# The last feed-forward of a four-layer decoder: one phase over all groups, the second weight quantised inside it, the result stored row by row

## The reference

```python
def fake_quant_weight(w, bits=8):
    qmax = 2.0 ** (bits - 1) - 1
    scale = jnp.max(jnp.abs(w)) / qmax
    return jnp.clip(jnp.round(w / scale), -qmax - 1, qmax) * scale

def qat_lora_linear(x, W, b, A, B):
    base = jnp.einsum('bsi,oi->bso', x, fake_quant_weight(W)) + b
    lora = jnp.einsum('bsr,or->bso', jnp.einsum('bsi,ri->bsr', x, A), B)
    return base + 2.0 * lora

h = qat_lora_linear(layernorm(x), W_fc, b_fc, A_fc, B_fc)          # 256 -> 1024
h = jax.nn.gelu(h, approximate=False)
x = x + qat_lora_linear(h, W_proj, b_proj, A_proj, B_proj)         # 1024 -> 256
```

## Time and profile before

| | us |
|---|---|
| median of 3 runs (3753.2 to 3757.0) | 3754.8 |
| the profiled execution | 3752.83 |
| its span, first to last instruction | 3751.0 |
| TensorE busy | 3235.7 (86%) |
| VectorE busy | 2180.4 (58%) |
| ScalarE busy | 1803.9 (48%) |
| GpSimd busy | 1012.5 (27%) |
| mean granted TensorE clock | 0.913 |

### The profile page before, as it was taken

How to read it: one execution, slowest core, us unless ns; L and a number is a source line. 1 busy time by engine, 2 the same in 40 slices (tenths; PEclk the granted TensorE clock), 3 DMA queues, 4 the chain that set the end, 5 groups by cost and what they waited for, 6 DMA issues and landing times. The chain is left out here.

```text
span 3751.0 us, 54988 instructions
## 1 busy us (share of the span) xinstructions
PE 3235.7 (86%) x18722; PEld 1868.1 (50%) x18722; DVE 2180.4 (58%) x4483; ACT 1803.9 (48%) x4177; POOL 1012.5 (27%) x1177
## 2 busy tenths in 40 slices
PE   6978639998859899967899989795899999998988
PEld 3655428887637566634455556363233333332745
DVE  5764445455555565575645447334788888884730
ACT  5956613333223244443544435212477777776521
POOL 2534544433421022232344332104011111111300
PEclk9988759999979899988888889897799999999989
DMA  9100045665430000042000031213100000001100
GB/s 336 56 9 1 1 195 189 204 190 170 146 93 2 12 1 1 1 131 80 1 1 1 1 140 53 108 55 123 39 13 14 18 18 18 18 10 47 46 0 23
DMA packets 160866, 240.51 MB, mean 64 GB/s; under 512 B 22531, under 2 KB 135812, under 8 KB 156708
## 3 DMA queue, kind: packets, MB, share of 16 engines
q1 hardware_dynamic: 146772, 199.27, 16.2%
q0 software_dynamic: 13824, 37.77, 3.1%
HBM read 131.97 MB, written 104.99 MB: 63 GB/s over the span
## 5 line engine op out<-in xcount | busy, mean ns | idle before, releaser
L4145 DVE TENSOR_REDUCE peaks<-ps 128x1 f32<-128x1024 f32 x512 | 609.0, 1221 | 149.3 <-PE ps L4091 144.0
L4173 ACT ACTIVATE attn<-ps 128x512 f32<-128x512 f32 x1024 | 536.6, 604 | 117.4 <-PE ps L4082 115.8
L4091 PE MATMUL ps<-keys,queries 96*128 96x512 bf16 x1024 | 396.9, 393 | 19.2 <-DMA keys<-parts 15.5
L4082 PE MATMUL ps<-queries,keys 99*128 99x512 bf16 x1024 | 390.4, 385 | 3.5 <-ACT attn L4173 2.7
L4104 PE MATMUL ps<-attn,head_values 128*32 128x512 f32 x2048 | 272.3, 604 | 0.0
L4082 PEld LDWEIGHTS ps<-queries,keys 99*128 99x128 bf16 x1024 | 99.1, 98 | 307.0 <-ACT attn L4173 222.7
L1930 PE MATMUL ps<-experts,tileT 128*128 x884 | 231.4, 384 | 5.2 <-issue 5.2
L1145 POOL TENSOR_TENSOR attn_w<-attn_w,attn_share 128x512 f32<-128x512 f32 x128 | 130.7, 1042 | 377.3 <-DVE attn_share L1014 377.3
L2133 DVE COPY normed<-ps 128x256 f32<-128x256 f32 x221 | 93.8, 424 | 205.7 <-PE ps L1946 108.1
L1848 POOL DMA_INDIRECT rows<-expert_rows,index x128 | 121.6, 950 | 197.8 <-DVE normed L2133 115.0
L1946 PE MATMUL ps<-experts,hiddenT 128*128 (+1 forms) x474 | 147.5, 393 | 28.9 <-DVE hiddenT L2142 25.3
(11 more groups left out here) (653 smaller groups left out, 7049.4 us busy)
## 6 DMA issues: line engine op xcount, KB each, us to landing
tile_in<-routed_rows SPq DMA_DIRECT2D x244, 128.0 KB, 2.2
expert_rows<-normed SPq DMA_DIRECT2D x221, 128.0 KB
routed_rows<-zeros SPq DMA_DIRECT2D x2, 8064.0 KB, 44.9
experts<-in_L_ffn_experts SPq DMA_DIRECT2D x4, 3072.0 KB
routed_rows<-zeros SPq DMA_DIRECT2D x1, 12160.0 KB, 61.2
kT<-L_xattn_keys SPq DMA_DIRECT2D x8, 1024.0 KB
v<-L_xattn_values SPq DMA_DIRECT2D x8, 1024.0 KB
experts<-in_L_ffn_experts SPq DMA_DIRECT2D x8, 1024.0 KB
```

The source lines that it names most:

```text
L4082: nc.tensor.matmul(bank(("score", n)), keys[h % 3][0:DEEP, sl(kt)], queries[h % 3][0:DEEP, sl(c, CHUNK)], start=True, stop=True).then_inc( ...
L4091: last = nc.tensor.matmul(k.ps[:, SB + p % PB, :], queries[h % 3][0:ROWS, sl(t)], keys[h % 3][0:ROWS, sl(c, CHUNK)], start=True, stop=True)
L4145: v.tensor_reduce(peaks[:, r % 2, i // 2, i % 2:i % 2 + 1], k.ps[:, at:at + 2, :], AX.XY, ALU.max).then_inc(s["maxed"], 1)
L4173: nc.scalar.activation(attn[:, n % RING, :], bank(("score", n)), ACT.Exp, scale=1.0 / 16.0).then_inc(s["read"], 1)
```

## The change

`l3_ffn` becomes one phase, "feed", with a program written out for each engine. The land phase, the quantise phase, the eight phases of the groups and the store phase in `build` are gone, and no loop is left.

- TensorE makes the four low-rank products of W_fc as soon as the weights are there, then turns and spreads the maximum of W_fc alone, transposes group 0 and makes its "up" products. For each later group g it makes all 8 transposes, then the "up" products of g, then the "down" products of g-1. In group 1 the maximum of W_proj is turned and spread and its eight low-rank products stand one behind each "up" product.
- VectorE takes the maximum of W_fc, the statistics of group 0, normalises it, quantises W_fc and adds its low-rank products; then the statistics of the other 12 rows at once, the maximum of W_proj, the normalising of group 1, and then it quantises W_proj and adds its low-rank products. Behind that it normalises group g+2 and adds the four rows of group g.
- ScalarE takes two roots (group 0; the other 12 rows, between the fifth and the sixth Gelu of group 0), copies both halves of the transposed group in one operation, and makes the Gelus. `hT` and `xT` exist twice.
- SyncE stores each of the 16 rows (128 KB) as soon as it is added, and waits for all at the end.
- "up" products go to banks 0 to 3, "down" and low-rank ones of W_proj to 4 and 5, transposes to 6 and 7. The bias product stands first in each "down" row instead of last.

```diff
@@ -2543,6 +2543,8 @@
     nc = k.nc
     INNER, RANK = 1024, 16
     M = INNER // P
+    CHUNK = 512
+    UP, DOWN, TURN = (0, 1, 2, 3), (4, 5), (6, 7)
     n = "L3_ffn_"
...
@@ -2553,74 +2555,211 @@
...
-        side_by_side(k, (land_part(k), 1))
...
-        LORA = [(0, kt, c) for kt in range(KD) for c in range(INNER // 512)] + [(1, m, 0) for m in range(M)]
...
-        side_by_side(k, (quantise, 1), (norm_part(k, 0, lambda kt: k.xT[:, kt, :], (4, 5)), 1))
...
-        def group(g, more):
-            gemm_phase(k, "up", [(P, GT, products([(wf[:, kt, sl(m)], k.xT[:, kt, :]) for kt in range(KD)]), "act", to_gelu(m))
-                                 for m in range(M)])
-            side_by_side(k, (gemm_part(k, "down", residual_jobs(k, g, hT, M, wp, bp), range(4)), 1),
-                         *([(norm_part(k, g + 1, lambda kt: k.xT[:, kt, :], (4, 5)), 1)] if more else []))
...
+        hT = [sb(k, stack, f"hT{i}", [P, M, GT]) for i in range(2)]
+        xT = [k.xT, sb(k, stack, "xT", [P, KD, GT])]
+        size, row_ = sb(k, stack, "size", [P, 2, 3]), sb(k, stack, "row", [1, 2, 2])
+        stats, moments = sb(k, stack, "stats", [P, BATCH, 6]), sb(k, stack, "moments", [P, BATCH, 2])
+        rstd = sb(k, stack, "rstd", [P, BATCH])
+        LORA_UP = [(kt, h) for h in range(INNER // CHUNK) for kt in range(KD)]
+        out = k.out.rearrange("b t d -> t b d")
+        names = ("step peaked turned maxed spread sized up_lora up_ready down_lora down_ready measured rooted normed xturned x_took "
+                 "up_made gelu_done down_made added stored")
+        with phase(k, "feed", names) as (block, s):
+            @block.sync
+            def _(sp):
+                fetch_next(k, sp)
+                for t in range(BATCH):
+                    sp.wait_ge(s["added"], t + 1)
+                    sp.dma_start(out[:, t, :], k.x[:, t, :]).then_inc(s["stored"], 16)
+                sp.wait_ge(s["stored"], 16 * BATCH)
+            @block.tensor
+            def _(pe):
...
+                def turn(g):
+                    if g >= 1:
+                        pe.wait_ge(s["x_took"], g)
+                    for j in range(GROUP):
+                        pe.wait_ge(s["normed"], g * GROUP + j + 1)
+                        for kt in range(KD):
+                            last = nc.tensor.transpose(k.ps[:, TURN[kt], sl(j)], k.normed[:, j, sl(kt)], k.ident[:, :])
+                    last.then_inc(s["xturned"], 1)
+                def lora_up(i):
+                    kt, h = LORA_UP[i]
+                    nc.tensor.matmul(k.ps[:, UP[i], :], af[:, sl(kt)], bfT[:, sl(h, CHUNK)], start=True, stop=True).then_inc(s["up_lora"], 1)
+                def lora_down(m):
+                    if m >= 2:
+                        pe.wait_ge(s["down_ready"], m - 1)
+                    else:
+                        pe.wait_ge(s["sized"], 2)
+                    nc.tensor.matmul(k.ps[:, DOWN[m % 2], 0:DIM], ap[:, sl(m)], bpT[:, :], start=True, stop=True).then_inc(s["down_lora"], 1)
+                def up(g, m):
+                    at = g * M + m
+                    if m == 0:
+                        pe.wait_ge(s["x_took"], g + 1)
+                    if g == 0 and m < 4:
+                        pe.wait_ge(s["up_ready"], 4 if m == 3 else max(2, m + 1))
+                    if at >= 4:
+                        pe.wait_ge(s["gelu_done"], at - 3)
+                    if g == 0 and m == 4:
+                        pe.wait_ge(s["up_ready"], 4)
+                    for kt in range(KD):
+                        last = nc.tensor.matmul(k.ps[:, UP[at % 4], :], wf[:, kt, sl(m)], xT[g % 2][:, kt, :], start=kt == 0, stop=kt == KD - 1)
+                    last.then_inc(s["up_made"], 1)
+                def down(g, j):
+                    at = g * GROUP + j
+                    if at == 0:
+                        pe.wait_ge(s["down_ready"], M)
+                    if at >= 2:
+                        pe.wait_ge(s["added"], at - 1)
+                    bank = k.ps[:, DOWN[at % 2], 0:DIM]
+                    nc.tensor.matmul(bank, k.ones[0:1, 0:P], bp[0:1, :], start=True, stop=False)
+                    for m in range(M):
+                        if j == 0:
+                            pe.wait_ge(s["gelu_done"], g * M + m + 1)
+                        last = nc.tensor.matmul(bank, hT[g % 2][:, m, sl(j)], wp[:, m, :], start=False, stop=m == M - 1)
+                    last.then_inc(s["down_made"], 1)
+                landed(k, pe)
+                for i in range(len(LORA_UP)):
+                    lora_up(i)
+                turn_peaks(0)
+                spread(0)
+                turn(0)
+                for m in range(M):
+                    up(0, m)
+                for g in range(1, GROUPS):
+                    turn(g)
+                    if g == 1:
+                        turn_peaks(1)
+                    for m in range(M):
+                        up(g, m)
+                        if g == 1:
+                            if m == 0:
+                                spread(1)
+                            else:
+                                lora_down(m - 1)
+                    if g == 1:
+                        lora_down(M - 1)
+                    for j in range(GROUP):
+                        down(g - 1, j)
+                for j in range(GROUP):
+                    down(GROUPS - 1, j)
+            @block.vector
+            def _(dve):
+                link = Link(dve, s["step"])
+                v = nc.vector
+                both = (wf, wp)
...
+                def peak_of_all(which):
+                    dve.wait_ge(s["turned"], which + 1)
+                    link(v.tensor_reduce(row_[:, which, 0:1], k.ps[0:1, DOWN[0], 0:P], AX.X, ALU.max))
+                    v.tensor_scalar(row_[:, which, 1:2], row_[:, which, 0:1], 1.0 / 127.0, None, ALU.mult).then_inc(s["maxed"], 1)
+                def quantise(which):
+                    w = both[which]
+                    dve.wait_ge(s["spread"], which + 1)
+                    v.tensor_copy(size[:, which, 1:2], k.ps[:, DOWN[1], 0:1]).then_inc(s["sized"], 1)
+                    dve.wait_ge(s["sized"], which + 1)
+                    link(v.reciprocal(size[:, which, 2:3], size[:, which, 1:2]))
+                    link(v.tensor_scalar(w[:, :, :], w[:, :, :], size[:, which, 2:3], MAGIC, ALU.mult, ALU.add))
+                    link(v.tensor_scalar(w[:, :, :], w[:, :, :], MAGIC, 127.0, ALU.subtract, ALU.min))
+                    link(v.tensor_scalar(w[:, :, :], w[:, :, :], -128.0, size[:, which, 1:2], ALU.max, ALU.mult))
+                def measure(tiles):
...
+                    link(v.tensor_scalar(rstd[:, these], moments[:, these, 1], LN_EPS, None, ALU.add))
+                    v.reciprocal(rstd[:, these], rstd[:, these]).then_inc(s["measured"], 1)
+                def normalise(g):
+                    dve.wait_ge(s["rooted"], min(g, 1) + 1)
+                    if g >= 1:
+                        dve.wait_ge(s["xturned"], g)
+                    for j in range(GROUP):
+                        t = g * GROUP + j
+                        v.tensor_scalar(k.normed[:, j, :], k.x[:, t, :], moments[:, t, 0:1], rstd[:, t:t + 1],
+                                        ALU.subtract, ALU.mult).then_inc(s["normed"], 1)
+                def add(g, j):
+                    t = g * GROUP + j
+                    dve.wait_ge(s["down_made"], t + 1)
+                    v.tensor_tensor(k.x[:, t, :], k.ps[:, DOWN[t % 2], 0:DIM], k.x[:, t, :], ALU.add).then_inc(s["added"], 1)
+                landed(k, dve)
+                peak(0)
+                measure(range(GROUP))
+                peak_of_all(0)
+                normalise(0)
+                quantise(0)
+                for i, (kt, h) in enumerate(LORA_UP):
+                    dst = wf[:, kt, sl(h, CHUNK)]
+                    dve.wait_ge(s["up_lora"], i + 1)
+                    v.scalar_tensor_tensor(dst, k.ps[:, UP[i], :], 2.0, dst, ALU.mult, ALU.add).then_inc(s["up_ready"], 1)
+                measure(range(GROUP, BATCH))
+                peak(1)
+                normalise(1)
+                peak_of_all(1)
+                quantise(1)
+                for m in range(M):
+                    dve.wait_ge(s["down_lora"], m + 1)
+                    v.scalar_tensor_tensor(wp[:, m, :], k.ps[:, DOWN[m % 2], 0:DIM], 2.0, wp[:, m, :], ALU.mult, ALU.add).then_inc(s["down_ready"], 1)
+                for g in range(GROUPS):
+                    if g + 2 < GROUPS:
+                        normalise(g + 2)
+                    for j in range(GROUP):
+                        add(g, j)
+            @block.scalar
+            def _(act):
+                def root(part, tiles):
+                    act.wait_ge(s["measured"], part + 1)
+                    nc.scalar.activation(rstd[:, tiles], rstd[:, tiles], ACT.Sqrt).then_inc(s["rooted"], 1)
+                def take_x(g):
+                    act.wait_ge(s["xturned"], g + 1)
+                    if g >= 2:
```

(53 more changed lines are left out.)

44 lines of the change are left out of this document (15 added, 29 removed).

## The result

The changed kernel took 3724.6 us as the median of 6 runs against 3755.3 for the kernel before: ratio 0.9924, interval 0.991 to 0.9938. That is 28.5 us by the ratio, and 30.7 us between the medians. A second comparison on another occasion gave 3727.1 and a ratio of 0.993 (0.9915 to 0.9944). The forecast was 23 us less, 3732, with a range of 3724 to 3742.

A forecast was written before the change was run, and what follows sets the result against it. TensorE's remaining products set the floor, with preparation, phase ends and the final store as removable costs. First "up" at 3581.7, last add at 3725.4, plus 2.6 tail: span 3728.0, 23.0 less than before, so 3732 us; range 3724 to 3742.

The forecast's parts named there:

- the head: From the cross-attention's last add to the first "up" product, at 3581.7 instead of 3593.7: 12.0 us earlier.
- the first "up": Group 0's eight "up" products: 13.8 us at full clock plus 2.5 for starting at half clock, 16.3 us.
- the boundaries: Between groups, transposes and an uncovered copy cost 2.4 us each, three times; one clock fall of 1.8 us allowed.
- the second group: Its "up" carries W_proj's spread and eight low-rank products: 21.2 us, then 0.6 waiting for the last add.
- the tail: Behind the last add, only the last row's 128 KB store is left: 2.6 us instead of 8.3.
- The 16-row products do not hold the clock: In the head, W_fc's low-rank stream won't keep full clock: three records at 0.43 us, five at 0.86.
- rival A: The clock falls at all three group boundaries, each costing 1.4 to 3.1 us: about 3738 us; chance 0.17.
- rival C: In the second group TensorE waits up to 4 us for VectorE or ScalarE's table loads: 3736 us; chance 0.08.
- The table loads: ScalarE's second root, among group 0's Gelus: two loads with two short operations take 2.9 us, without drain gaps.
- Rival B: At the end, the last row lands no sooner than the whole store did, 7.5 us: 3737.5 us; chance 0.07.
- D: Groups don't overlap; each "up" waits as long as the barriers did: 3745 us; chance 0.04.
- E: Half clock from the second group's boundary, held by 16-row products into its "down": slower, 3774.5 us; chance 0.02.

The follow-up runs named there:

- e3: Changed kernel with each group's "down" products right behind its own "up" products, group overlap undone; last feed-forward stage 156.3 us against 154.6.
- e9: Changed kernel with transposes one step earlier, bias added on VectorE and W_proj's low-rank products in pairs; last feed-forward stage 137.5 us against 154.6.
- e5: Changed kernel with a second, unneeded copy of 1024 columns ahead of the needed one at each group boundary; last feed-forward stage 160.7 us against 154.6.
- e7: Changed kernel with each group's transposes one step earlier; last feed-forward stage 151.3 us against 154.6.
- e6: Changed kernel with five unread full-row products in TensorE's idle time before the first "up"; last feed-forward stage 154.0 us against 154.6.
- e2: Changed kernel with W_proj also quantised and its low-rank products added ahead of the first "up"; last feed-forward stage 161.5 us against 154.6.
- e1: Changed kernel with one 2 MB store at the end in place of 16 row stores; last feed-forward stage 160.4 us against 154.6.
- e10: As e9, with five unread full-row products before the first "up"; median 3704.1 us, ratio 0.9867 to the kernel before, last feed-forward stage 133.6 us.

## Why the prediction was right, step by step

The time fell within the range, at its low edge, and the mechanisms held, except that the clock never fell at a boundary. That the first median fell inside the range by 0.6 us is in part luck; the second is 3.1 us inside. The stage was forecast 6.0 us too long: 1.8 in the head, 0.4 in the first "up", 0.7 in the boundaries, 1.8 for the fall, 0.8 in the second group and 0.5 in the tail. Each can be read.

- **The head** was forecast at 14.3 and was 12.5. The term that was mis-sized is the time at which the clock falls, which I took from the one trace of before (1.9 us behind the last add by its row, read as 2.0). After, it fell at 3.1:

```profile
3565.00:3566.00 1.00, 1.00 (x3) 0.39 (x2) 1.00 (x5) 0.00 (x0) 0.00 (x0) 0.78 0.00 0
3566.00:3567.00 1.00, 1.00 (x2) 0.00 (x0) 0.93 (x7) 0.00 (x0) 0.00 (x0) 0.50 0.00 0
```

  In the twelve traces of the experiments it fell at 1.9 twice and at 3.0 to 3.5 ten times. Where it was 1.9, the head was 13.65 (e3, e9), 0.7 under the forecast. In e3 the peaks are read and scaled 6.6 us into the stage, where the forecast had 7.2 (the end of the stream, the turning and the reading each 0.1 to 0.3 shorter), and normalising took 0.1 less. The wait of VectorE was 1.51 there, near the forecast's 1.8:

```profile
3570.55 0.28 DVE L2671 TENSOR_REDUCE row<-ps 1x1 f32<-1x128 f32 x1 [1.51 <-PE ps L2580]
```

  So the mechanism of the stream was right, and its size was one of two cases.
- **The 16-row products do not hold the clock**: it fell while they ran, 2.8 us after the first one began. This step held.
- **The first "up"**: 15.9 us against 16.3. The price of a slow start came from the four "up" stretches of before, of which I wrote that all start at half clock. In the trace the first two do; in the third and the fourth the clock falls 1.0 and 0.8 us behind their first product.
- **Boundaries**: 2.15 against 2.4 each, and none of three fell, where I had let one fall (1.8) and had given rival A, all three, a chance of 0.17. I had compared 2.4 with 2.65, and had named the bias product at the end of each "down" before as an argument against A without adding its 0.6 us to the stretch. Before, it lay between the last full-row product and the "up" product at 3631.36:

```profile
3628.14 0.69 PE L243 MATMUL ps<-L_ffn_b_proj,ones 1*128 1x256 f32 x2
3628.77 0.44 PE L365 MATMUL ps<-ident,normed 128*128 128x128 f32 x2
```

  So the stretches of before were 3.0 to 3.2 us (3.07 in e5, where one in three fell). The change made them 1 us shorter, 0.6 of it by the bias product, which now stands at the front of the row. The Trainium skill, "TensorE: Matmul & The Clock Gate", "Part 4: PE-mode transpose", has transposes as no work for the clock, and by that all three could have fallen; none did, and no run takes transposes alone. That the shorter stretch saved the boundaries fits these rows (0 of 27 falls at 2.15, 1 of 3 at 3.07, 3 of 3 at 3.0 to 3.2), but e7's 3.9 us without a fall speaks against a rule by length alone, and so do the falls of e5 and e6 behind 2.3 us. It stays open, and with it the cause of the 6 us that e2 puts down to the clock.
- **The second group**: 21.0 and a wait of 0.5 inside it against 21.2 + 0.6. The nearest row, the bias product, gave the price of a 16-row one within 0.03 (0.82 against 0.85), and the last two, which stood together, cost 1.12 and not 1.7. Quantising under the "up" products was covered, rival C fell.
- **The table loads** took no more than in the earlier trace rows: load, root, load, Gelu in 2.8 us.

```profile
3586.63 1.28 ACT L2737 ACT_TABLE_LOAD   x1
3587.93 0.21 ACT L2737 ACTIVATE rstd<-rstd 128x12 f32<-128x12 f32 x1
3588.16 1.28 ACT L2751 ACT_TABLE_LOAD   x1
3589.45 1.26 ACT L2751 ACTIVATE hT<-ps,L_ffn_b_fc 128x512 f32<-128x512 f32 x2
```

  By the drain of 1.38 us for each switch that the Trainium skill gives in "ScalarE: Activation LUTs", "What ACT_TABLE_LOAD costs", it would have been 5.6, an estimate; the trace shows no such gap and decides.
- **The tail**: landing 1.7 as in the nearest row, where I had taken 2.0, and 0.2 us less around it than allowed. Rival B fell; e1 shows that the 5.8 us are the landing alone.
- **D and E** fell. E needed the clock held down through the second group's "up"; it was 1.00 throughout, in every trace.

## What to carry to other kernels

Where one stage quantises or prepares several weights ahead of its first product, try leaving only the one that the first product reads there: here moving the other cost half of what it brought, and it was still a gain. Once a stage is one chain on TensorE, cost every record of it: products with few rows paid twice their records whenever they stood alone between full ones, and moving 16 of them to VectorE brought more (13 us) than any other step behind the change. A fall of the clock among the products behind the first "up" cost 1.7 us each time in these kernels, and it came only behind stretches of 2.3 us or more without full-row products; whether it comes could not be told from the length of the stretch, so keep it in the range, not in the sum.

## What the runs showed of the hardware that I had not expected

- The moment at which the clock falls behind the same code was one of two, 1.9 or 3.0 to 3.5 us after the last add, and this alone moves the stage by 1.7 us between executions (e3).
- Five full-row products whose result nobody reads raised the clock 2.4 us after the first of them and took 2.1 us off the first "up" (e6; 2.4 us in e10 too).
- The clock fell behind a stretch of 2.3 us of few-row products in which TensorE was idle for only 0.5 (2 of 7 traces), at 1.7 us each, and held through one of 3.9 us (e7).
